# Attention values of two quads of heads: one piece of 48 products per quad in place of 32 and 16

## What is computed

```python
scores = jnp.einsum('bhqd,bhkd->bhqk', Q, K) / jnp.sqrt(jnp.float32(D_K))
scores = jnp.where(mask == 0, jnp.float32(-jnp.inf), scores)
attn = jax.nn.softmax(scores, axis=-1)
ctx = jnp.einsum('bhqk,bhkd->bhqd', attn, V)
...
x = x + jnp.tanh(g_xattn[0]) * _L0_xattn_ref(_layernorm(x, axis=-1), ctx_1024, ctx_1024, mask_Bx1xSxS2_ik0, L0_xattn_W_q, L0_xattn_W_k, L0_xattn_W_v, L0_xattn_W_o)
x = x + jnp.tanh(g_ffn[0]) * _L0_ffn_ref(_layernorm(x, axis=-1), L0_ffn_gate_w, L0_ffn_w_gate, L0_ffn_w_up, L0_ffn_w_down)
```

## Time and profile before

| | before |
|---|---|
| median of three runs | 1772.78 us |
| the profiled execution | 1771.65 us |
| its span | 1769.9 us |
| PE busy | 1702.7 us (96%) |
| DVE busy | 1037.8 us (59%) |
| ACT busy | 834.9 us (47%) |
| values (L1362 on PE) | 1536 products, 323.7 to 761.3 us |

### The profile page before, as it was taken

How to read it: one execution, slowest core, us unless ns; L and a number is a source line. 1 busy time by engine, 2 the same in 40 slices (tenths; PEclk the granted TensorE clock), 3 DMA queues, 4 the chain that set the end, 5 groups by cost and what they waited for, 6 DMA issues and landing times.

```text
span 1769.9 us, 28536 instructions
## 1 busy us (share of the span) xinstructions
PE 1702.7 (96%) x10502; PEld 1515.3 (86%) x10502; DVE 1037.8 (59%) x1779; ACT 834.9 (47%) x1490; POOL 234.2 (13%) x306
## 2 busy tenths in 40 slices
PE   7999999999999999949999999999999999999995
PEld 6898898778877887628999999999999999999995
DVE  6666567888898889744535435345354354453541
ACT  3232225878887788714424334344244243342430
POOL 0000001222233223120002002020020020100101
PEclk9999999999999999968999999999999999999998
DMA  7554546766665666224335335344353353443421
GB/s 256 211 204 177 209 157 214 189 161 182 181 187 158 177 186 177 68 95 144 108 108 149 107 107 148 107 123 132 107 146 102 103 154 112 115 135 110 119 95 21
DMA packets 76797, 253.85 MB, mean 143 GB/s; under 512 B 11136, under 2 KB 11136, under 8 KB 75424
## 3 DMA queue, kind: packets, MB, share of 16 engines
q1 hardware_dynamic: 64704, 218.48, 38.6%
q0 software_dynamic: 12000, 34.14, 8.2%
HBM read 189.14 MB, written 52.43 MB: 136 GB/s over the span
## 4 chain that ended last, share of the span: by engine, by line
PE 54%; POOL 0%; issue 0%; DMA 0%; DVE 0%; DVEq 0%; ACT 0%; POOLq 0%
PE gu_ps L1667 12%; PE gu_ps L1666 12%; PE gu_ps L1665 12%; PE y_ps L1684 6%; PE y_ps L1682 6%; PE y_ps L1683 6%; PE y_ps L1693 1%; PE gu_ps L1651 1%; POOL out L1528 0%; DMA xg<-xn_rows,both_i 0%; POOL xg L1518 0%; DVE y_cols L1627 0%; PE gu_ps L1711 0%; DVE y_sb L1605 0%; DVEq L1476 0%
## 5 line engine op out<-in xcount | busy, mean ns | idle before, releaser
L1665 PE MATMUL gu_ps<-xs_hi,ws_hi 128*128 128x448 f32 x1024 | 371.1, 362 | 1.4 <-DVE xs_lo L1600 1.4
L1667 PE MATMUL gu_ps<-xs_hi,ws_lo 128*128 128x448 f32 x1024 | 372.4, 364 | 0.0
L1666 PE MATMUL gu_ps<-xs_lo,ws_hi 128*128 128x448 f32 x1024 | 372.1, 363 | 0.0
L1595 DVE TENSOR_TENSOR ws_lo<-w_raw,ws_hi 128x1024 fp32r<-128x1024 f32 x189 | 231.8, 1227 | 185.1 <-ACT ws_hi L1547 183.5
L1547 ACT ACTIVATE ws_hi<-w_raw 128x1024 fp32r<-128x1024 f32 x189 | 198.4, 1050 | 146.6 <-PE y_ps L1684 146.6
L908 ACT ACTIVATE sm<-sm,least 112x752 f32<-112x752 f32 x256 | 234.0, 923 | 4.8 <-DVE least L1022 4.7
L1022 DVE CUSTOM_DVE_ANT_0 sm<-m_ps,mq 112x752 f32<-112x752 f32 x256 | 229.4, 932 | 3.1 <-PE m_ps L1322 1.7
L1338 PE MATMUL t_ps<-cst,sm 112*128 112x112 f32 x1536 | 216.6, 264 | 3.5 <-ACT e_t L915 1.7
L1338 PEld LDWEIGHTS t_ps<-cst,sm 112*128 112x128 f32 x1536 | 176.4, 142 | 43.1 <-issue 27.8
L1665 PEld LDWEIGHTS gu_ps<-xs_hi,ws_hi 128*128 128x128 f32 x1024 | 192.5, 188 | 15.1 <-issue 1.7
L1666 PEld LDWEIGHTS gu_ps<-xs_lo,ws_hi 128*128 128x128 f32 x1024 | 193.0, 188 | 14.3
(11 more groups left out here) (159 smaller groups left out, 2430.5 us busy)
## 6 DMA issues: line engine op xcount, KB each, us to landing
w_raw<-wstream SPq DMA_DIRECT2D x192, 512.0 KB
ks<-k_split SPq DMA_DIRECT2D x192, 192.0 KB, 3.4
k_split<-k_split SPq DMA_DIRECT2D x32, 768.0 KB, 3.3
v_rows<-v_out SPq DMA_DIRECT2D x16, 768.0 KB, 4.9
vs<-v_rows SPq DMA_DIRECT2D x16, 768.0 KB, 6.8
c_raw<-ctxT SPq DMA_DIRECT2D x7, 1504.0 KB, 10.8
qs<-q_hi POOLq DMA_DIRECT2D x64, 112.0 KB, 3.0
mq_raw<-maskq SPq DMA_DIRECT2D x7, 656.2 KB, 6.4
```

Source lines behind the costliest of these rows:

```text
L1595: nc.vector.tensor_tensor(w_lo[s][:], w_raw[s][:], w_hi[s][:], ALU.subtract).then_inc(wlo_done[s], 1)
L1665: nc.tensor.matmul(o, w_hi[s][:, w], xs_hi[:, c], start=(c == 0), stop=False)
L1666: nc.tensor.matmul(o, w_hi[s][:, w], xs_lo[:, c], start=False, stop=False)
L1667: mm = nc.tensor.matmul(o, w_lo[s][:, w], xs_hi[:, c], start=False, stop=(c == DC - 1))
```

## The change

Both quads whose values were made in two pieces get one piece each, at the later of the two turns. Quad 1 (counted from 0) was made in turns 10 (chunks 0 to 3) and 11 (chunks 4 and 5), quad 2 in turns 13 and 15.

```diff
-V_CHUNKS = {1: (0, KC), 7: (0, KC), 10: (0, 4), 11: (4, KC), 13: (0, 4), 15: (4, KC)}
+V_CHUNKS = {1: (0, KC), 7: (0, KC), 11: (0, KC), 15: (0, KC)}
```

## The result

The changed kernel takes 1811.28 us, the median of four runs from 1804.73 to 1814.30, against 1773.30 us before (four runs, 1771.05 to 1774.73): a ratio of 1.0212, 95% interval 1.0183 to 1.0241. It is slower, as forecast, but by 38 us in place of 22, and outside the range, which ended at 1808. Its four runs lie 9.6 us apart and those of before 3.7; the mean granted clock goes with that spread (0.969 to 0.975 over the four runs).

A forecast was written before the change was run, and what follows sets the result against it. PE was taken to bound a batch, ACT turns 10 and 13. Six middle batches at 2.85 us (17.1), the first 2.5 and the last 2.6 sum to 22.2 us more: median 1795.0 us, range 1781 to 1808.

The forecast's parts named there:

- What bounds it: Attend: PE is the bound over a middle batch (57.88 of 58.07 us), but turns 10 and 13 are full on ACT.
- Turn 10, 0.42 us come back: Middle batch, turn 10: of the removed piece's 1.66 us only 0.42 return, because PE waits for ACT's copy.
- Turn 12 begins 1.38 us late: Middle batch: turn 11's lead shrinks to 0.13 us, its longer piece adds 1.51, so turn 12's first tile is 1.38 late.
- Turn 13 returns 0.04: Middle batch: removing the piece from turn 13 returns 0.04 us, as ACT's copy holds turn 14's first tile.
- −0.04 + 1.51: Quad 2's terms in a middle batch: 0.04 us returned in turn 13, 1.51 us more in turn 15.
- A batch of 60.9 us: Sign in the profile after: a middle batch takes 60.9 us from one turn 1 to the next.
- DVE's cx late by about 1.1 us: Sign in the profile after: DVE's cx of quad 1 has about 1.1 us of idle time ended by o_ps.
- clock 1.00 outside of two places: Sign in attend: the granted clock stays at 1.00 except at the two places where it falls now.
- The clock falls: Rival, 14%: in attend the clock falls behind 4 of the 16 waits, 13.6 us more, 1808.6 us.
- PE alone counts: Rival, 4%: only PE's own time matters, so 16 mergings save 0.24 us each, 3.8 us in all, 1769.0 us.
- half comes back: Rival, 11%: one of the two places has unseen slack, so a batch loses 1.4 us, 11 us in all, 1784.

The follow-up runs named there:

- Quad 2 alone: Against the kernel before, only quad 2 is made in one piece, at turn 15, and quad 1 keeps its two pieces; 1787.85 us, ratio 1.0083.

## Why the prediction was right and wrong

- **What bounds it: right.** PE over a batch, ACT in turns 10 and 13. The run with the pieces left out shows it best.
- **Turn 10, 0.42 us come back: right.** From the last tile of turn 10 to the first of turn 11 it was to take 1.71 us, and takes 1.74; the wait was put at 1.3 and is 1.19.
- **Turn 12 begins 1.38 us late: right.** From the first tile of turn 10 to that of turn 12 it takes 8.80 us (453.81 to 462.61), and took 7.47: 1.33.
- **Turn 13 returns 0.04: right.** From its last tile to the first of turn 14, 2.09 was forecast, 2.15 is there and 2.13 was: next to nothing either way. Quad 2 alone makes a batch 1.47 longer, as −0.04 + 1.51 says.
- **A batch of 60.9 us, DVE's cx late by about 1.1 us, clock 1.00 outside of two places.** The first is exact where the clock holds. DVE's wait for cx is 1.27 us. The third is wrong.
- **"The clock falls", at 14%: the step that failed.** The profiled execution has eight new falls and they cost 20.2 us, nearly as much as the waits; the sum had them at nothing. The rival's own price was 4 falls of 3.4 us, 13.6 in all; measured were eight of 2.5 on average (4.9 us where a stretch lasted 10 us, 4.6 for a pair), so half the number and too high a price partly made up for each other. The fall was set beside the forecast as an unlikely addition, when it should have been a term of the sum. The row for it was on the table: a wait of 1.49 us and 6.8 us at 0.50 behind it. Against it I put that the clock held 1.00 through turns 8 to 10, "but without waits as long". That is no evidence: those turns have no waits of that size, and the change makes sixteen. The nearest row to a wait of 1.2 to 1.6 us was that of 1.49. With its 4 falls the forecast would have been 1808.6; the median of four runs was 1811 and that of two later ones 1805. That this lies close is partly luck, by the two errors just named.
- **The rule on transposes** in the Trainium skill (TensorE: Matmul & The Clock Gate, Part 4: PE-mode transpose), by which this case was the likely one, points the right way here. But the clock also held 1.00 over whole batches (and those of 60.88 us), with turns 8 to 10 in them, in which PE makes mostly transposes; so they aren't enough for a fall by themselves. That transposes are the reason is not shown: no run replaced them with other work.
- **PE alone counts (1769), and half comes back (1784): both wrong.** The rule of the Trainium skill (Perfetto Trace Analysis, Identifying the Most-Contended Engine) to work first on the engine of highest occupancy would have led to the first, if PE's busy time is taken as its occupancy. The same section of the Trainium skill says that matmul busy time doesn't measure how much TensorE has left, and goes by its weight loads instead; these were busy for 46.73 of 58.07 us, less than DVE's 51.77. Moving PE's own time around gained nothing, because in the turns concerned it was not PE that set the pace.

What stays open: why the clock falls behind one wait of 1.6 us and not behind the next. Eight of 16 did in one execution of the changed kernel and three in another; over the six profiles that have such waits (1.04 to 1.72 us) it is 22 of 72. Also open is whether the wait itself counts or the missing products, since every run with such waits at turns 11 and 14 lacks them too; the changed kernel with one exponential between the copies, which lacks them and has no long wait there, speaks for the wait, by one profile.

## What to carry to other kernels

Work that fills an engine's waiting time is free only where it stands. Before moving it, cut the windows turn by turn and look which engines have no gap in the turn that it leaves and in the turn that it goes to; a mean over a batch hides both. And where such a move opens waits of a microsecond or more on TensorE, as here, count the clock as a term of the sum: doing work for nothing in the gap (1795 us) was cheaper here than leaving it empty (1811).

## What the runs showed that was not expected

Up to the last batch the clock fell behind waits of 1.04 to 1.6 us and behind none of up to 0.8 us, though the sum of the waits was nearly the same (19.2 and 22.8 us). And a fall isn't fixed by the program: near 318 us PE's wait of 1.49 us brought it in the first profile of the changed kernel and left it out in the second.

In the last batch, though, it also fell where PE had next to no gap. There turn 14 has no scores, and behind its tiles stand the logits, 16 products that are only 8 columns wide. Windows around them, in the run with all 48 products early (a wait of 0.25 us ends at 760.0, and the logits begin at 760.45):

```profile
758.00:760.00 2.00, 1.75 (x28) 1.06 (x20) 0.21 (x1) 1.42 (x4) 0.39 (x1) 1.00 0.03 8
760.00:762.00 2.00, 1.99 (x21) 2.00 (x21) 0.42 (x1) 0.54 (x1) 0.00 (x0) 1.00 0.00 0
762.00:764.00 2.00, 2.00 (x4) 0.81 (x5) 0.52 (x3) 0.00 (x0) 0.00 (x0) 0.56 0.28 37
```

PE is shown busy for 3.74 of the 4 us ahead of the fall. So a fall doesn't need a gap that the profile shows. Nor do these rows suffice for one: in the last batch of the kernel before nearly the same rows stand, and the clock stays at 1.00 from there to 768 us.

```profile
748.42 0.60 PE L1338 MATMUL t_ps<-cst,sm 112*128 112x112 f32 x4 [0.26 <-ACT e_t L915]
748.86 1.65 PE L1302 MATMUL w_ps<-gw_sb,xT 128*112 128x8 f32 x16
```

What decides it was not tested.
